# A graph network on one core: copies of x1 as the start of the second sums, issued by ScalarE, and a subtraction on GpSimd

## What is computed

```python
# layer 0: normalised aggregation
deg = segment_sum(w_all, dst_all); d = rsqrt(deg)
out = segment_sum((x @ W)[src_all] * (d[src_all] * w_all * d[dst_all])[:, None], dst_all)
x1 = layernorm(x + relu(out + b))
# layer 1: messages from x1[dst], filtered by the edge's attributes, summed by src
S_agg, V_agg = segment_sum(messages(x1[dst], filter(edge_attr)), src)
S = shifted_softplus(S_agg @ W1_s) @ W2_s
V = (V_agg @ W1_v) @ W2_v
y = layernorm(x1 + concatenate([S, V]))
```

## Time and profile before

| | |
|---|---|
| median of 3 runs | 1081.26 us (1080.84 to 1082.22) |
| profiled execution | 1074.51 us |
| its span | 1072.7 us |
| TensorE busy | 920.3 us, 86% |
| VectorE busy | 846.7 us, 79% |
| ScalarE busy | 707.3 us, 66% |
| GpSimd busy | 652.9 us, 61% |
| DMA | 280.39 MB, mean 261 GB/s |

### The profile page before, as it was taken

How to read it: one execution, slowest core, us unless ns; L and a number is a source line. 1 busy time by engine, 2 the same in 40 slices (tenths; PEclk the granted TensorE clock), 3 DMA queues, 4 the chain that set the end, 5 groups by cost and what they waited for, 6 DMA issues and landing times.

```text
span 1072.7 us, 17283 instructions
## 1 busy us (share of the span) xinstructions
PE 920.3 (86%) x4812; PEld 743.0 (69%) x4812; DVE 846.7 (79%) x2396; ACT 707.3 (66%) x1642; POOL 652.9 (61%) x945
## 2 busy tenths in 40 slices
PE   7889888999973999999999389999999999915553
PEld 7767777777753888887888268888887888714443
DVE  7688888886824788788889578888888888719997
ACT  4669877777761566666666446666666666638886
POOL 4028888888851566666666345776677676426665
PEclk9989999998995999999999789999999999955555
DMA  9989999999998499999998767999999999688995
GB/s 350 418 274 250 242 237 240 239 240 242 236 224 279 165 341 324 327 315 313 323 323 311 273 187 178 216 206 218 226 217 211 216 228 189 94 220 337 389 400 233
DMA packets 121443, 280.39 MB, mean 261 GB/s; under 512 B 13746, under 2 KB 38342, under 8 KB 121350
## 3 DMA queue, kind: packets, MB, share of 16 engines
q1 hardware_dynamic: 73590, 186.25, 47.9%
q0 software_dynamic: 35280, 82.63, 40.0%
q10 hardware_dynamic: 12480, 10.42, 3.0%
HBM read 132.38 MB, written 146.87 MB: 260 GB/s over the span
## 4 chain that ended last, share of the span: by engine, by line
PE 43%; DVE 11%; DMA 8%; issue 4%; ACT 2%; POOL 1%; SPq 1%; ACTq 0%; DVEq 0%; POOLq 0%
PE bank L1309 8%; PE bank L1357 7%; PE bank L1340 6%; PE bank L1371 5%; DVE stat L1167 4%; PE bank L1313 4%; PE bank L1369 3%; DMA edge_mem<-x 3%; PE bank L1334 3%; PE bank L1300 2%; PE bank L1367 2%; DMA G_mem<-x 2%; PE bank L1346 2%; DVE node_mem L1158 1%; DVE stat L1043 1%
## 5 line engine op out<-in xcount | busy, mean ns | idle before, releaser
L548 POOL DMA_INDIRECT sum<-R_mem,sidx_all x79 | 129.1, 1634 | 85.0 <-DMA sum<-zeros 48.7
L609 POOL DMA_INDIRECT sum<-R_mem,l_sidx x79 | 135.6, 1717 | 45.9 <-issue 21.9
L595 POOL DMA_INDIRECT G_mem<-x_d,dst_i x79 | 77.2, 977 | 90.9 <-PE bank L1344 64.3
L1309 PE MATMUL bank<-G_hi 128*128 128x512 f32 x316 | 131.4, 416 | 0.0
L1309 PE MATMUL bank<-G_lo,G_hi 128*128 128x512 f32 x316 | 124.9, 395 | 0.0
L1225 PE MATMUL bank<-G_hi,M_mem 128*128 128x512 f32 x200 | 86.3, 432 | 7.0 <-ACT R_mem L681 6.4
L1313 PE MATMUL bank<-G_hi,G_lo 128*128 128x512 f32 x316 | 85.3, 392 | 0.0
L1114 DVE SCALAR_TENSOR_TENSOR edge_mem<-edge_mem,Y,bank 128x128 f32<-128x128 f32 x237 | 71.2, 385 | 15.0 <-ACT edge_mem L806 15.0
L1340 PE MATMUL bank<-edge_mem,Winv 128*128 128x512 f32 x158 | 81.8, 600 | 0.1
L1225 PE MATMUL bank<-G_lo,M_mem 128*128 128x512 f32 x200 | 80.5, 402 | 0.0
L1387 PE MATMUL bank<-ident,node_mem 128*128 128x128 f32 x80 | 27.5, 447 | 61.5 <-DVE node_mem L1158 61.5
(11 more groups left out here) (230 smaller groups left out, 2831.5 us busy)
## 6 DMA issues: line engine op xcount, KB each, us to landing
node_mem<-sum SPq DMA_DIRECT2D x41, 512.0 KB, 5.9
filt_d<-node_mem SPq DMA_DIRECT2D x40, 512.0 KB, 4.9
node_mem<-filt_d SPq DMA_DIRECT2D x79, 256.0 KB, 4.9
sum<-zeros SPq DMA_DIRECT2D x33, 512.0 KB, 14.2
G_mem<-x SPq DMA_DIRECT2D x20, 512.0 KB, 6.9
x_d<-node_mem SPq DMA_DIRECT2D x20, 512.0 KB, 3.5
edge_mem<-x SPq DMA_DIRECT2D x19, 512.0 KB, 6.1
x_d<-R_mem SPq DMA_DIRECT2D x19, 512.0 KB, 3.9
```

The source lines that it names most:

```text
L548: pool.indirect_dma_start(sum0, bass.IndirectOffsetOnAxis(ap=sidx[:, t:t + 1], axis=0), R[t % 8][:, :], None, compute_op=ALU.add).then_inc ...
L595: pool.indirect_dma_start(G3[t % 8][:, :], None, x1_d, bass.IndirectOffsetOnAxis(ap=dst_i[:, t:t + 1], axis=0)) \
L609: pool.indirect_dma_start(sum1, bass.IndirectOffsetOnAxis(ap=l1_sidx[0:n, t:t + 1], axis=0), R3[t % 8][0:n, :], None, compute_op=ALU.add). ...
L1309: pe.matmul(bank[4 + a][:, :], zT_hi[a][:, c * P:(c + 1) * P], w[c][:, :], start=(c == 0 and w is W0h), stop=False)
```

## The change

`sum1` begins as a whole copy of x1. The zeros for its columns 0 to 127 go, and the copy of a pair is one store of 512 KB. ScalarE issues those of pairs 0 to 35 in the node stage, one tile later than it scales the pair; SyncE issues the last four once gather 7 of the edge stage has landed. Since columns 0 to 127 of the sums now hold x1 as well, GpSimd subtracts the kept columns in the last stage, ahead of ScalarE's first operation on the pair. VectorE scales the last two tiles and not the last alone. SyncE issues one row load and one filter load ahead of the last two stores of x1, and the other three of each behind them. TensorE multiplies zeros three times between the last scatter of layer 0 and the node stage. ScalarE's wait for `rows_st[4]` to `rows_st[7]` ahead of the edge stage is kept as it is.

```diff
@@ SyncE
                 if j >= 6:
                     i = j - 6
-                    sp_.wait_ge(n_x1, min(2 * i + 2, TR - 1))
-                    if i == T2 - 1:
-                        sp_.wait_ge(n_last, 1)
+                    sp_.wait_ge(n_x1, min(2 * i + 2, TR - 2))
+                    if i >= T2 - 2:
+                        sp_.wait_ge(n_last, i - T2 + 3)
                     sp_.dma_start(layer_pair(x1_d, i, 0, D), in_pair(res2[i % 8], i, 0, D)).then_inc(n_st[i % 8], 16)
-                    for k in ((i,) if i < T2 - 2 else (i - 1, i) if i == T2 - 1 else ()):
-                        sp_.dma_start(layer_pair(sum1, k, C, D), in_pair(res2[k % 8], k, C, D)).then_inc(rows_st[k % 8], 16)
+                    if i == T2 - 3:
+                        sp_.wait_ge(n_tr, TR)
+                        trow_in(0)
+                        filt_in(0)
+
+            def sum1_out(k):
+                sp_.dma_start(layer_pair(sum1, k, 0, D), in_pair(res2[k % 8], k, 0, D)).then_inc(rows_st[k % 8], 16)
 
             for j in range(T2 + 6):
                 nodes0(j)
+            for t in range(1, 4):
+                filt_in(t)
+                trow_in(t)
+            sp_.wait_ge(f_gather[7], 16)
+            for k in range(T2 - 4, T2):
+                sum1_out(k)
@@ GpSimd
-                        pool.wait_ge(s_zero1, 16 * (T2 + 4))
+                        pool.wait_ge(s_zero1, 16 * 4)
...
+            pool.wait_ge(n_keep, TR)
+
+            def nodes1(s):
+                if live(s, 0, T2):
+                    b = s % NA
+                    pool.wait_ge(g_al[b], 16 * (s // NA + 1))
+                    pool.tensor_tensor(al[b][:, :, 0:C], al[b][:, :, 0:C], xs[s][:, :, :], ALU.subtract).then_inc(g_agg, 1)
+                if live(s, 6, T2):
+                    t, a = s - 6, (s - 6) % 4
...
@@ ScalarE
-                    if t2 % 2 == 0:
-                        z = layer_pair(sum1, t2 // 2, 0, C)
-                        act.dma_start(z, zeros[:, 0:z.shape[1] * C].rearrange("p (k c) -> p k c", c=C)).then_inc(s_zero1, 16)
...
-                    if t8 < TR - 1:
+                    if t8 < TR - 2:
                         act.activation(r, r, ACT.Identity, bias=tiny[b][:, 6, k:k + 1], scale=tiny[b][:, 5, k:k + 1]).then_inc(n_x1, 1)
                 if live(s, 11):
                     t9 = s - 11
...
+                    if t9 % 2 and t9 // 2 < T2 - 4:
+                        k = t9 // 2
+                        act.dma_start(layer_pair(sum1, k, 0, D), in_pair(res2[k % 8], k, 0, D)).then_inc(rows_st[k % 8], 16)
...
                 if live(s, 0, T2):
-                    act.wait_ge(g_al[s % NA], 16 * (s // NA + 1))
+                    act.wait_ge(g_agg, s + 1)
@@ VectorE
-            dve.wait_ge(n_root, 2 * K_RSTD)
-            r = res[(TR - 1) % 16]
-            dve.tensor_scalar(r, r, w[:, 5, 0:1], w[:, 6, 0:1], ALU.mult, ALU.add).then_inc(n_last, 1)
+            for t in (TR - 2, TR - 1):
+                g, k, r = t // 2, t % 2, res[t % 16]
+                dve.wait_ge(n_root, K_RSTD * (g - T2 + 3))
+                dve.tensor_scalar(r, r, tiny[g % 4][:, 5, k:k + 1], tiny[g % 4][:, 6, k:k + 1], ALU.mult, ALU.add).then_inc(n_last, 1)
@@ TensorE
+            def keep_clock(b, n):
+                for _ in range(n):
+                    pe.matmul(bank[b][:, :], zeros[:, 0:P], zeros[:, 0:512], start=True, stop=True)
...
+            pe.wait_ge(e_scat, 16 * TR)
+            keep_clock(7, 3)
```

More of the change, by code:

```diff
@@ L365, in build @@
         g_al = [sem(f"g_al{i}") for i in range(NA)]
+        g_agg = sem("g_agg")
         g_soft = sem("g_soft")
@@ L377, in build @@
         rows_st = [sem(f"rows_st{i}") for i in range(8)]
[L379 to L387, removed]
         NZ = 8
@@ L400, in build, with in_pair @@
         K_RES4, K_MV4, K_RSTD = 3, 2, 4
+        def in_pair(tile, j, c0, c1):
+            return tile.rearrange("p (k d) -> p k d", k=2)[:, 0:min(2, TR - 2 * j), c0:c1]
         block = ctx.enter_context(nc.Block())
@@ L442, in _ @@
             sp_.wait_ge(e_lo, T)
-            def in_pair(tile, j, c0, c1):
-                return tile.rearrange("p (k d) -> p k d", k=2)[:, 0:min(2, TR - 2 * j), c0:c1]
             def x_in(j):
@@ L565, in nodes0 @@
                     st.mark(pool.tensor_scalar(w[:, 7, :], mean, -1.0, None, ALU.mult))
-                    held(pool, n_rs, 2 * (g + 1))
+                    pool.wait_ge(n_rs, 2 * (g + 1))
                     st.mark(pool.tensor_tensor(w[:, 3, :], w[:, 2, :], w[:, 2, :], ALU.mult))
@@ L569, in nodes0 @@
                     st.mark(pool.tensor_tensor(w[:, 4, :], w[:, 3, :], w[:, 0, :], ALU.mult))
-                    held(pool, n_rstd, st.reached())
+                    pool.wait_ge(n_rstd, st.reached())
                     st.mark(pool.tensor_scalar(w[:, 3, :], w[:, 4, :], -0.5, 1.5, ALU.mult, ALU.add))
@@ new lines, in nodes1 @@
+            def nodes1(s):
[5 more added lines that the diff above has]
+                    t, a = s - 6, (s - 6) % 4
+                    w, st = tiny4[a], Stage(g_rstd, t, K_ROOT)
+                    pool.wait_ge(g_mv, K_MV4 * (t + 1))
+                    st.mark(pool.tensor_scalar(w[:, 0, :], mv4[a][:, :, 1], EPS, None, ALU.add))
+                    st.mark(pool.tensor_scalar(w[:, 7, :], mv4[a][:, :, 0], -1.0, None, ALU.mult))
+                    pool.wait_ge(g_rs, 2 * (t + 1))
+                    st.mark(pool.tensor_tensor(w[:, 3, :], w[:, 2, :], w[:, 2, :], ALU.mult))
+                    st.settle(pool)
+                    st.mark(pool.tensor_tensor(w[:, 4, :], w[:, 3, :], w[:, 0, :], ALU.mult))
+                    st.settle(pool)
+                    st.mark(pool.tensor_scalar(w[:, 3, :], w[:, 4, :], -0.5, 1.5, ALU.mult, ALU.add))
+                    st.settle(pool)
+                    st.mark(pool.tensor_tensor(w[:, 5, :], w[:, 3, :], w[:, 2, :], ALU.mult))
+                    st.settle(pool)
+                    st.mark(pool.tensor_tensor(w[:, 6, :], w[:, 7, :], w[:, 5, :], ALU.mult))
@@ L631, in _ @@
+            for s in range(T2 + 6):
+                nodes1(s)
         @block.scalar
@@ L780, in nodes0 @@
                     t9 = s - 11
-                    if t9 < TR - 1:
+                    if t9 < TR - 2:
                         act.wait_ge(n_x1, t9 + 1)
                     else:
-                        act.wait_ge(n_last, 1)
+                        act.wait_ge(n_last, t9 - TR + 3)
+                    if t9 % 2 and t9 // 2 < T2 - 4:
+                        k = t9 // 2
+                        act.dma_start(layer_pair(sum1, k, 0, D), in_pair(res2[k % 8], k, 0, D)).then_inc(rows_st[k % 8], 16)
                     act.copy(xs1[t9 // 2][:, t9 % 2 * C:(t9 % 2 + 1) * C], res[t9 % 16][:, 0:C]).then_inc(n_keep, 1)
@@ L828, in edges1 @@
                     t, a = s - 2, (u - 2) % 8
-                    held(act, f_gather[a], 16 * (turn(t, a, 8) + 1))
+                    act.wait_ge(f_gather[a], 16 * (turn(t, a, 8) + 1))
                     wait(act, f_tr, t - 3)
```

6 lines of the change are left out of this document (removed).

## The result

The changed kernel took **1102.56 us** (median of 4 runs, 1099.38 to 1105.63), the kernel before 1081.36 in the same session: a ratio of **1.0195, 95% interval 1.0165 to 1.0225**. A second session gave 1101.9 against 1078.57, 1.0212 [1.0186, 1.0239]. The change makes the kernel slower by some 22 us; the forecast was 1109.2, and the range 1093 to 1121 holds the result.

A forecast was written before the change was run, and what follows sets the result against it. TensorE bounds node and edge stages, DMA fills the gap between, VectorE leads the last stage; -1.9 + 13.6 + 16.2 = +27.9 us gives 1102.4 profiled, 1109.2 median, range 1093 to 1121.

The forecast's parts named there:

- Part 2: Start of the node stage: three matmuls of zeros raise TensorE's clock before real work; -1.9 us, bounds +1.0 and -2.3.
- Part 1: Node stage, steady part: ScalarE's 512 KB copies replace zeros and SyncE's 384 KB copies, same bytes; at most 0.75 us, taken as 0.
- Parts 3 and 4: Gap before edge stage: last stores land earlier (-2.3 us alone), but ScalarE waits for four late copies; together +13.6 us.
- Part 5: Last stage: 40 GpSimd subtractions make GpSimd the bound, 3.15 us a pair against VectorE's 2.65; +16.2 us.
- rows 12: Last-stage profile rows: small GpSimd operations starting during VectorE's two-SBUF-input step or scaling take 0.29 and 0.36 us, not 0.20.
- A: Last stage: GpSimd's need stays hidden within 2.65 us a pair; +12.5 us in all, 1093.8; chance 0.10.
- B: Gap: copies land by 613.7 and cost nothing; 1077.9 with GpSimd hidden, chance 0.03; 1093.3 with the forecast last stage, 0.04.
- C: Last stage: VectorE operations of two kinds stop GpSimd for their full length, 3.79 us a pair; +48.4 in all, 1129.7; chance 0.08.
- D: Gap and node start: gathers and copies compete (+18 us), the clock does not answer (+1); +35.2 in all, 1116.5; chance 0.07.

## Why the prediction was right, and where it was not

**Part 2, zeros.** Forecast -1.9; the table has -1.5, the run without them about 1 us. Right in kind; the price leaned on the one execution of the kernel before in which the clock rose late.

**Part 1, node stage.** This step failed: "Cost or gain at most 0.75; I take 0", with TensorE's own work as the cover. The table has +5.0 behind tile 1. I read the cover from a trace in which ScalarE's queue carried only 128 KB pieces, counted the bytes, found them the same, and did not ask whose transfer waits when the copies get a queue of their own. The cover was thinner than TensorE's 0.75 us of idle time made it look: eight loads of x already stood in the chain of waits of the same profile, with little room to become longer. The run with SyncE's copies removes the loss.

**Parts 3 and 4, the gap and the wait.** -1.7 and +15.3 are +13.6, as forecast. Gather 7 stood 8.9 behind the first, landing took 3.82 (3.7 taken), from there to the projection 6.1 (6.8 taken); the projection stood 18.8 behind the first gather, 19.4 in the forecast. The run with the late wait confirms it by itself with -13.1.

**Part 5, the last stage.** The mechanism was there, the size was not: +3.9 for +16.2. A subtraction took 0.726 (0.74 taken). The sum of needs was the mis-sized term: 3.15 a pair were expected, 2.76 measured. Two items of it: I put 0.08 between all eight instructions, but L622 starts 0.04 before the one ahead of it ends and L614 0.05 before, which saves 0.25 a pair (why these two alone wasn't tried); and of the locks I took some 0.32, but the rows lose 0.05 + 0.16 = 0.21. 3.15 less 0.25 and 0.11 is 2.79. Over 32 pairs the 0.11 between 2.76 and 2.65 is 3.5 us, and 0.6 is the start, 4.1 for the 3.6 to 4.0 measured; the run with six small operations shows that this is GpSimd's length and no new wait. Of the signs I gave, 3.15 a pair and a VectorE that waits for ScalarE did not show. And rows 12 were read a little too strictly: GpSimd lost 0.09 of the 0.24 that was left of VectorE's operation and 0.14 of 0.31, so less than the part that is left.

**Rivals.** A (GpSimd hidden, +12.5) was nearer to the last stage's truth than my forecast, but by another road: nothing was hidden, the overrun was only 0.11 a pair. B, the faster side, fell with the wait, as expected. C is refuted; but I had tied it too loosely to the lock of which the Trainium skill tells ("SBUF — State Buffer", section "SBUF: two separate sides"): a lock held for the whole instruction costs the later operation what is left of the earlier one, not its full length, so the period of 2.76 does not speak against it. D's late start did not come.

**The total** was 24.9 for 27.9 between the profiled executions, and it is closer than its parts, which is luck: 12.3 too much in the last stage stand against 5.0 too little in the node stage, 0.4 for the zeros, and 3.8 in the scatter phase and the tail behind the edge stage. Of those last, the first varies by 6.5 between executions of one kernel, and the second between 13.9 and 16.3 over all traces; I can't give either to the change. The median came out 6.6 under the 1109.2: 3.0 of that is this sum, and 3.6 the difference of 6.75 between median and profile that I carried over unchanged; for the changed kernel it was 3.2.

## What to carry to other kernels

When the work a wait counts moves later, move the wait to the first use that it guards: here an inherited wait at the head of a stage turned four late copies into 13 us. Before giving stores a queue of their own, look at which loads share the DMA engines with them: equal bytes are not equal times for the transfer that the busiest engine needs. And where an engine gets close to the pace of another, add up its real rows, overlaps included, before calling it the bound: 0.4 us a pair too much in the sum made 16 us out of 4.

## What was unexpected in the hardware

- A stream of 512 KB stores issued by ScalarE took the landing of SyncE's loads of x from 6.1 to 6.9 us in the two executions before to 7.1 to 8.2 in the two of the changed kernel, at no more bytes. On SyncE's own queue the same stores landed in 4.5 (6.2 on ScalarE's) and the loads in 6.3 and 6.4.
- VectorE and GpSimd settled to a common period, 2.76 us, in which neither shows a wait: what each yields to the other lies inside the durations (0.53 for 0.41, 0.38 for 0.22), so a timeline without waits is no proof of an engine's own need.
- TensorE's granted clock, at 0.50 when the node stage began, rose after different amounts of like work: behind seven of tile 0's matmuls in one execution of the kernel before, behind two in the other. That is 1.1 us of tile 1's start without any edit.
